# A decoder layer on one core: the order of the first weight loads, and the order of work in expert round 0

## The reference

```python
# 1. attention, one head of 512: three softmaxes over the same scores
raw = Q K^T * scale
out = (softmax(causal raw) V + softmax(Q Kc^T) Vc + softmax(top-64 of raw, else 0) V) / 3
x = x + out Wo + bo
# 2. cross-attention, 8 heads of 32, over channels first, with relative positions in a window of 4
# 3. product-key experts
q = x Wq^T ; sim = q . keys            # 2 x 8 heads x 128 keys for each token
row = 128 * argmax(sim x) + argmax(sim y) ; gate = relu(max + max)   # one row per head
hidden = gelu(x W_in^T + sum_h (x . in_a[row_h]) gate_h * in_b[row_h])
out    = hidden W_out^T + sum_h (hidden . out_a[row_h]) gate_h * out_b[row_h]
```

## Time and profile before

| | us |
|---|---|
| median of 3 runs | 2641.53 (2639.85 to 2643.36) |
| the profiled execution's own time | 2653.43 |
| its span, first to last instruction | 2651.6 |
| attention pass, up to the expert pass's first loads | about 1475 |
| PE / DVE / ACT / POOL busy | 2402.3 / 2056.3 / 1091.2 / 1117.3 |
| mean granted clock of TensorE | 0.977 |

### The profile page before, as it was taken

One profiled execution on the slowest core, in us unless ns is written; L12 is line 12 of the kernel. 1 busy time (PEld: TensorE's weight loads), 2 busy tenths in 40 slices (PEclk: granted clock), 3 DMA queues, 4 the chain that ended last, 5 costly groups with the idle time before them and its releaser, 6 DMA issues. The chain is left out here.

```text
span 2651.6 us, 40533 instructions
## 1 busy us (share of the span) xinstructions
PE 2402.3 (91%) x12792; PEld 1322.9 (50%) x12792; DVE 2056.3 (78%) x5959; ACT 1091.2 (41%) x2559; POOL 1117.3 (42%) x1534
## 2 busy tenths in 40 slices
PE   7889999999999999999986799999999999999975
PEld 4456556566565665566554344444444444444432
DVE  0466776767767676677654289999999999999997
ACT  2256666666666666666665021111111111111110
POOL 1133333333333333333332245555555556655552
PEclk9999999999999999999998899999999999999997
DMA  3044545445454454545544789999999999999996
GB/s 107 22 117 129 167 138 157 135 134 172 144 157 130 135 169 149 149 133 142 159 150 141 281 326 382 383 384 383 385 384 387 390 385 385 381 385 382 382 374 248
DMA packets 301699, 639.22 MB, mean 241 GB/s; under 512 B 163120, under 2 KB 164144, under 8 KB 301488
## 3 DMA queue, kind: packets, MB, share of 16 engines
q0 software_dynamic: 83968, 438.34, 43.8%
q1 hardware_dynamic: 183728, 97.63, 13.0%
q10 hardware_dynamic: 33792, 100.67, 11.3%
HBM read 586.19 MB, written 150.99 MB: 278 GB/s over the span
## 5 line engine op out<-in xcount | busy, mean ns | idle before, releaser
L1099 DVE CUSTOM_DVE_ANT_0 scores<-s_bank,added 128x512 f32<-128x512 f32 x512 | 350.2, 687 | 232.4 <-PE s_bank L593 185.9
L1401 PE MATMUL l_bank<-fold,xn_tf 128*128 128x512 f32 x1024 | 453.6, 596 | 10.2 <-ACT xn_tf L1473 6.8
L1375 POOL DMA_INDIRECT out_rows<-rows_out,rows_now x256 | 313.7, 1226 | 313.2 <-DVE res L1633 235.3
L909 ACT ACTIVATE probs<-scores,nmx 128x512 f32<-128x512 f32 x512 | 373.2, 729 | 105.8 <-DVE nmx L1099 100.4
L526 POOL TENSOR_TENSOR added<-mask_add,band 128x136 f32<-128x136 f32 (+1 forms) x512 | 247.3, 485 | 341.9 <-DVE nmx L1099 340.7
L915 ACT COPY prob_t<-t_bank 128x512 f32<-128x512 f32 x512 | 299.4, 585 | 206.3 <-PE t_bank L603 205.5
L1369 POOL DMA_INDIRECT in_rows<-rows_in,rows_now x256 | 310.4, 1213 | 158.5 <-DVE hid L1605 91.0
L1486 ACT COPY sims<-l_bank 128x512 f32<-128x512 f32 x128 | 74.2, 580 | 623.7 <-PE l_bank L1401 610.5
L1401 PEld LDWEIGHTS l_bank<-fold,xn_tf 128*128 128x128 f32 x1024 | 195.8, 192 | 256.8 <-issue 249.5
L603 PEld LDWEIGHTS t_bank<-ident,probs 128*128 128x128 f32 x2048 | 236.0, 142 | 175.5 <-issue 122.3
L603 PE MATMUL t_bank<-ident,probs 128*128 128x128 f32 x2048 | 317.9, 281 | 5.0 <-ACT prob_t L915 2.7
(11 more groups left out here) (182 smaller groups left out, 3652.1 us busy)
## 6 DMA issues: line engine op xcount, KB each, us to landing
rows_in<-in_in_b_dram ACTq DMA_DIRECT2D x16, 2048.0 KB, 9.3
rows_out<-in_out_a_dram ACTq DMA_DIRECT2D x16, 2048.0 KB, 9.0
rows_in<-in_in_a_dram ACTq DMA_DIRECT2D x16, 1024.0 KB, 8.2
rows_out<-in_out_b_dram ACTq DMA_DIRECT2D x16, 1024.0 KB, 5.5
x_scratch<-x SPq DMA_DIRECT2D x32, 512.0 KB, 7.6
rel_scratch<-rel_pad SPq DMA_DIRECT2D x16, 640.0 KB, 3.0
band<-rel_scratch SPq DMA_DIRECT2D x512, 20.0 KB, 2.3
prob_scratch<-probs SPq DMA_DIRECT2D x512, 20.0 KB, 2.4
```

The lines of the kernel that those rows point to most:

```text
L909: nc.scalar.activation(prob_tile(s % PSLOTS), scores[:, s % 2, :], ACT.Exp, bias=nmx[:, s:s + 1], scale=-1.0, accum_out=lsum[:, s:s + 1]). ...
L1099: nc.vector.tensor_tensor_reduce(out=scores[:, s % 2, :], in0=s_bank[s % HPT][:, 0:L], in1=added[:, s % 2, :], scale=-1.0, scalar=-NEG, op ...
L1375: nc.gpsimd.indirect_dma_start(out_rows[:, h, :], None, rows_out, bass.IndirectOffsetOnAxis(rows_now[:, odd, h:h + 1], 0)).then_inc(out_lo ...
L1401: ins = nc.tensor.matmul(l_bank[c % 2][:], xn_t[:, k, :], fold[:, k, c * BANK:(c + 1) * BANK], start=(k == 0), stop=(k == KD - 1))
```

## The change

In the attention pass, Wq is SyncE's first transfer with a semaphore of its own, and Wk is ScalarE's first transfer with another; TensorE waits for each where it turns it. `first_in` now counts the seven columns alone. ScalarE's scaling of cb_q and its drain come behind `fold_scores` instead of ahead.

In expert round 0 alone, TensorE runs heads_in(0) ahead of all four chunks of similarities(2) (instead of after three), ScalarE runs diagonals(0) first and the GELU between chunks 1 and 2 (instead of after chunk 3), and VectorE does gate_rest and the six sum_in first and then the whole search of round 2. All other rounds are as before.

```diff
-        weights = [(w_q, w["attn_Wq"]), (w_k, w["attn_Wk"]), (w_v, w["attn_Wv"]), (w_o, w["attn_Wo"]),
+        weights = [(w_v, w["attn_Wv"]), (w_o, w["attn_Wo"]),
...
-        N_EARLY = 2
-        N_FIRST_DMAS = N_EARLY + len(columns)
+        N_FIRST_DMAS = len(columns)
...
         def _(sp):
+            sp.dma_start(w_q, w["attn_Wq"].rearrange("(k p) n -> p k n", p=P)).then_inc(wq_in_place, 16)
             for tile, src in columns:
                 sp.dma_start(tile[:], src).then_inc(first_in, 16)
...
             def fold_scores():
-                pe.wait_ge(first_in, 16 * N_FIRST_DMAS)
+                pe.wait_ge(wq_in_place, 16)
                 turn_weight("TQ", w_q)
+                pe.wait_ge(wk_in_place, 16)
                 turn_weight("TK", w_k)
...
+            act.dma_start(w_k, w["attn_Wk"].rearrange("(k p) n -> p k n", p=P)).then_inc(wk_in_place, 16)
+            act.wait_ge(consts, N_CONSTS)
+            fold_scores()
             act.wait_ge(first_in, 16 * N_FIRST_DMAS)
-            act.wait_ge(consts, N_CONSTS)
             nc.scalar.mul(cb_qs[:], cb_q[:], XSCALE)
             self_wait(act)
-            fold_scores()
...
             def step(r, slot):                                  # TensorE
+                ahead = 0 if r == 0 else 3
                 if not nothing_after(r, 2):
-                    similarities(r + 2, range(0, 3))
+                    similarities(r + 2, range(0, ahead))
                 heads_in(r, slot % 2)
                 if not nothing_after(r, 2):
-                    similarities(r + 2, range(3, CHUNKS))
+                    similarities(r + 2, range(ahead, CHUNKS))
...
             def step(r, slot):                                  # ScalarE
+                if r == 0:
+                    diagonals(0)
+                    similarities(2, range(0, 2))
+                    hidden(0)
+                    similarities(2, range(2, CHUNKS))
...
                 products_in(r, slot)                            # VectorE
-                if nothing_after(r, 2):
+                if r == 0 or nothing_after(r, 2):
                     gate_rest(r, slot)
                     for h in VE_HEADS:
                         sum_in(r, h)
+                    if r == 0:
+                        search(2, range(CHUNKS))
```

More of the change, by code:

```diff
@@ L275, in attention_pass @@
         acc = acc_bank[:, 0:P]
+        wq_in_place = sem("wq_in_place")
+        wk_in_place = sem("wk_in_place")
         first_in = sem("first_in")
@@ L330, in attention_pass @@
                    (cb_o, w["xattn_bo"])]
-        N_EARLY = 2
-        N_FIRST_DMAS = N_EARLY + len(columns)
-        N_REST_DMAS = len(weights) - N_EARLY + 1 + HPT + H
+        N_FIRST_DMAS = len(columns)
+        N_REST_DMAS = len(weights) + 1 + HPT + H
         N_CONSTS = 6
@@ L359, in _ @@
         def _(sp):
+            sp.dma_start(w_q, w["attn_Wq"].rearrange("(k p) n -> p k n", p=P)).then_inc(wq_in_place, 16)
             for tile, src in columns:
                 sp.dma_start(tile[:], src).then_inc(first_in, 16)
-            for n, (tile, src) in enumerate(weights):
-                sp.dma_start(tile, src.rearrange("(k p) n -> p k n", p=P)).then_inc(
-                    first_in if n < N_EARLY else rest_in, 16)
+            for tile, src in weights:
+                sp.dma_start(tile, src.rearrange("(k p) n -> p k n", p=P)).then_inc(rest_in, 16)
             sp.dma_start(b_o[:], w["attn_bo"].partition_broadcast(P)).then_inc(rest_in, 16)
@@ L1507, in step @@
             def step(r, slot):
[L1508 to L1513, removed]
+                if r == 0:
[3 more added lines that the diff above has]
+                    similarities(2, range(2, CHUNKS))
+                else:
+                    if not nothing_after(r, 2):
+                        similarities(r + 2, range(0, 2))
+                    diagonals(r)
+                    if not nothing_after(r, 2):
+                        similarities(r + 2, range(2, CHUNKS))
+                    hidden(r)
                 if not nothing_after(r, 2):
```

## The result

| | median us | ratio to before, 95% interval |
|---|---|---|
| before, 7 runs | 2641.35 (2639.85 to 2643.36) | |
| the changed kernel, 7 runs | 2649.64 (2647.38 to 2652.87) | 1.0028 [1.0018, 1.0039] |

The changed kernel is slower by 7.4 us of 2641 by the ratio (4.8 to 10.3), 8.3 us by the medians. 2640.7 was forecast, with a range up to 2646.0: wrong, and on the other side of zero. The profiled execution took 2647.38 us, its span 2645.6: *less* than the 2651.6 us of the profile of before. So the two profiles, laid side by side, say the opposite of the timed runs. That was the first thing to explain.

A forecast was written before the change was run, and what follows sets the result against it. VectorE was taken to set the pace in the expert pass, TensorE following with 1.85 us to spare in a round. -3.35 (weights) and +2.5 (expert round 0) gave -0.85 us: 2640.7 us, range 2635.5 to 2646.

The forecast's parts named there:

- Part 1: Weight loads at the start of the attention pass: TensorE starts earlier, less late scaling and drain, -3.35 us in sum.
- So TensorE starts at 10.4, 3.65 us earlier: Start of the kernel: weights landed by 10.1 us, constants at 10.33, so the first transpose moves from 14.06 us.
- rival (c): Start: GpSimd's drain waits for x_in, landing 3 us later; constants at 13.4 us, net +2.1, 2643.6 us; 10%.
- the table load in front of the first copy: ScalarE at the start: first copy of a turned bank 0.3 us late, caught up over three banks, costing nothing.
- Part 2: Expert round 0 in its new order: TensorE starts late and VectorE waits for heads_in(1) in round 1, +2.5 us.
- 4.3 us of late start: TensorE in expert round 0: heads_in(0) needs VectorE's gated lin, so work starts at 1531.3 us, 4.3 us later.
- about the surcharge of a start from idle, 12.42 - 10.46: TensorE in heads_in(0): starting from idle adds about 1.96 us to its 3.6 us, so it ends at 1536.9.
- rival (b): TensorE between similarities(1) and heads_in(0): idling costs more than the start wins, net +1.2 to +2.0, 2643.1 us; 28%.
- That execution is 11.9 us above the median; I take the difference off: Whole kernel: profiled 2653.43 us against timed median 2641.53; the difference is subtracted from 2652.6, giving 2640.7 us.
- Rival (a): Expert rounds 0 and 1: VectorE's wait, up to 5.64 us, is really won; net -5 to -9, say 2635.5; 14%.

The follow-up runs named there:

- part2_warm: The new order of expert round 0 alone, plus six useless TensorE products ahead of heads_in(0), against the kernel before: 2641.15 us, ratio 1.0001.
- part2_ahead1: The new order of expert round 0 alone, but with chunk 0 of similarities(2) ahead of heads_in(0) on TensorE, against the kernel before: 2639.55 us, ratio 0.9992.
- null: The kernel before, unchanged, timed and profiled again: 2643.25 us, ratio 1.0002.
- part1: The changed weight loads in the attention pass alone, against the kernel before: 2645.12 us, ratio 1.0005.
- part2: The new order of expert round 0 alone, weight loads as before, against the kernel before: 2648.15 us, ratio 1.0016.
- part1_xlate: The changed weight loads alone, with GpSimd's two loads of x issued behind the constants, against the kernel before: 2639.56 us, ratio 0.9987.

## Why the prediction was wrong

**Part 1, the step "So TensorE starts at 10.4, 3.65 us earlier".** Wq's landing was near enough (10.7 us against 10.1), the constants were wrong. They were taken to stay at 10.33 us; they came at 15.8. The cause is rival (c), to which 10% was given, and which was sized too small: x landed 5.5 us later, not 3, because the three loads took until 12.8 us and not 10.1. The row that was held against it, a drain of 4.49 us at the end of the attention pass with no GpSimd transfer in flight, is real but says nothing of this place: behind 0.2 us of clearing and no transfers a drain takes 0.26 us. The coincidence in the start's own rows, drain ends as x lands, was worth more than a like-named instruction 1460 us away. -3.35 us was forecast; by the profiles it is +2.1, timed +1.3 (-0.8 to +3.7). A smaller term, the table load in front of the first copy, was put at nothing and costs 0.25 us of it.

**Part 2, waits right, one cost left out.** +2.5 us was forecast, +4.4 by the profiles, timed +4.2. Each wait of VectorE in the new order came nearly as worked out, and so did the 4.3 us of late start. What failed is the old order, the yardstick: "about the surcharge of a start from idle, 12.42 - 10.46", charged to both orders. In the four other profiles with the old order TensorE idles 1.37 us there and its 24 products take 10.57 us, no surcharge; only the new order pays it. That is rival (b), at 28%, which had named this very condition and gave part 2 as 4.5 to 5.3 us. part2_warm splits the 4.4: 2.2 us clock, 2.3 us late start. Of (b)'s sign only the first half came: the clock is low in most of heads_in(0), but similarities(2) run at full rate (32 products in 13.90 us).

**The base.** "That execution is 11.9 us above the median; I take the difference off." That 11.9 us was a warning. 6.5 of it were the stop, at the very place the change touches, and can't be subtracted as a constant.

**Chances.** (b) and (c) were weighed one by one and joined only for the range's end, at +4.9 us. Both came true, and with the sizes above they make +6.5 us by the profiles, +7.4 timed, past the 5.3 us that counted as slower, to which 0.07 was given.

**Rival (a)** fell: in the changed kernel VectorE waits 2.28 us in round 1, and even where TensorE hardly idles (part2_ahead1) only 1.1 of the 6.0 us won at the first sum are left by round 1 and by finish 29.

## What to carry to other kernels

Before an idle engine is given work sooner, add up the engine that feeds it: if that one is busy from here to the next meeting point, an earlier hand-over is mostly a later wait. A gap opened in front of that engine costs what its slack doesn't cover (here 2.3 of 4.3 us), and the lower clock on top (2.2 us). GpSimd's drain here lasted until the last transfer that GpSimd had issued had landed; put the transfers behind such a drain. If the profiled execution is far above the median, take a second profile before reading 2 us out of it.

## What was not expected

- *TensorE's speed at a short place differs from execution to execution.* 16 transposes of Wk take 1.97 us in null and 3.67 in part1, the same instructions on the same data. (The table by stretch gives a granted clock of 1.00 for both, so that it is the clock there is a guess from the factor of nearly two.) At 118 us the profile does show it: the four products of mix with v take 3.68 us in the changed kernel, at a granted clock of 0.53, and 1.98 in part2_warm, at 1.00. Both rows are TensorE's timeline, the changed kernel first:

```profile
118.15 3.68 PE L572 MATMUL a_bank<-v,mix_t 128*128 128x512 f32 x4 [0.67 <-ACT mix_t L879]
```

```profile
118.76 1.98 PE L571 MATMUL a_bank<-v,mix_t 128*128 128x512 f32 x4 [0.68 <-ACT mix_t L877]
```

  The Trainium skill, "TensorE: Matmul & The Clock Gate", "What's actually happening", calls the moment of the change variable from run to run; these profiles agree. It is the likely, not a shown, reason why null's 12 runs spread over 8 us: the mean granted clock of the run falls from 0.982 in the shortest (2641.05 us) to 0.977 in the longest (2648.96).
- *The end of the attention pass moves by itself.* From about 1273 us (the last sum but two into x1) to the fold load, the profiles take 202.6 us (before), 202.7 (null), 199.1 (part1), 202.3 (part2), 198.6 (after), 199.0 (part2_warm) and 205.3 (part1_xlate), in code that none of these changes. With the 6.5 us of the stop in the profile of before, it is why the after profile was the shorter of the two in spite of both losses; the cause stays open.
- *The price of this drain is what GpSimd has in flight*: 0.26, 5.7 and 11.1 us for the same instruction.
